# A recurrence beside attention: state rows scanned in pairs, some input products made earlier, and fewer ballast matmuls between the products of a step

## The chip, the cores and the metric

One Trainium2 chip, one core. The metric is the device time of the whole kernel in microseconds. Inputs are 8 sequences of 512 tokens.

## The reference, cut to what matters

```python
h = tok(x)                                  # four attentions of 8 wide heads, (8, 512, 128)
h = h + attn_block(layernorm(h))
h = h + ffn(layernorm(h))
...
x_norm = _ln(x, norm_g, norm_b)             # in attn_block, H = 256, D = 128
xin = jnp.einsum('bsd,hd->sbh', x_norm, W_in)
def res_step(prev, xt):
    new = jnp.tanh(xt + prev @ W_res.T)
    new = LEAK * new + (1.0 - LEAK) * prev  # LEAK = 0.95
    return (new, new)
_, res_states = jax.lax.scan(res_step, h0, xin)
Bm = jnp.einsum('bsd,hd->bsh', x_norm, W_B)
A_bar = jnp.exp(A * delta[..., None])
B_bar = Bm * (1.0 - A_bar) / (A + 1e-08)
def ssm_step(prev, ab_bb): ...              # h = ab * prev + bb, over 512 positions
return readout(res_states) * gate + readout(ssm_states) * (1.0 - gate)
```

`readout` is a layer norm over H, a product with W_ro (128 x 256), and a Gelu.

## The kernel before, in words

The work is cut into 32 tiles of 128 positions of one sequence; tile j is sequence j % 8 of quarter j // 8. Everything is written out in Python, so each engine's order is the order of the calls in its block. The recurrence has 512 steps, which can't be shortened or run side by side. They are grouped into 32 bodies of 16 steps, (t, i) being step t of body i (STEPS, BODIES).

- **Before the steps**: loads, projections and attention of the first eight tiles.
- **Bodies 0 to 23**: 16 steps each, with one tile of attention, its norm and its gate per body beside them. AHEAD = 9 tiles lead.
- **Body 24** (FIRST_DECAY): beside the steps, PE spreads delta over partitions (`spread_delta`, L1680), ACT makes the decays (`decay`, L702), and the scans of the SSM begin.
- **Bodies 25 to 31** (FIRST_READ on): four readout tiles per body, one per four steps, and the rest of the SSM.
- **Tail**: the last eight tiles' readouts at their several stages (`rest_of_readouts`, with `alone=True`).

**A step** (`scan` on each engine). PE adds to a slot of PRE, which already holds the input's part (`fill`): eight products with y16 (four with res_hi, four with res_lo), one with kp's upper half, then 112 columns of zeros (L1490, bodies 0 to 23 only; ballast that adds nothing), four with y_lo, one with kp_lo (L1494). ACT then makes y16 (L637), the f32 state (L638) and kp (L640) from PRE; DVE makes y_lo (L1041) and kp_lo (L1045 or L1048); and the next step begins. PE's other ballast (`pads`, L1529) stands behind the step at hand-set sizes.

**States and their sums.** The leak makes the read state a sum over all earlier ones with factor KEEP = 0.05. ACT writes raw tanh values to `ys`, 16 rows (two halves of H by 8 sequences) of 513 columns, 2052 bytes, each. DVE makes sums in place with one scan per row and quarter (`sigma_row`, L1114): quarters 0 and 1 in bodies 8 to 23, quarter 2 in bodies 24 to 29. The last quarter is done in parts by `half` (64 columns, bodies 28 to 31), `third` (32, body 31) and 32 more a row in the tail, all at L1152, into the places of h_all and gate_all that SP has moved away to `h_last` and `gate_last` (L385 to L396).

**The SSM.** For each of 64 rows, PE makes the input product into PSUM (`feed` on PE, L1669, 128 x 128 f32), DVE multiplies it (`feed_scaled`, L1273) and scans (`recur`, L1289; L1283 and L1286 in the last quarter). Twelve rows are fed in body 24, the others two steps apart from body 25 on. c is the group of eight rows; quarter 0 is c = 0 and 1, 16 rows.

**A readout tile** goes through five stages, `u` being the step within it: PE turns and multiplies the sums (L1691 to L1694), ACT squares (L728), POOL makes the deviation (L513, L516, `r_dev`), DVE scales (L1251), ACT applies Gelu (L717), POOL blends (L539, L540, L502, L506), DVE takes moments (L1320, L1323), POOL their root (L524 to L530), ACT writes (L710), SP stores. On DVE, in a step: `scan`, then `sigma`, then L1251, `recur` or `feed_scaled`, then L1320 at u = 1, which waits for POOL's L506.

```python
                zeros = 112 if i < FIRST_DECAY else 0
                if zeros:
                    t_.matmul(PS[:, t % 2, 0:zeros], ident16[:, :], ballast[:, 0:zeros], start=False, stop=False, skip_group_check=True)
```

## Time and profile before

| | us |
|---|---|
| Three runs | 614.6 (median), 613.83, 616.22 |
| The profiled execution's own time | 613.99 |
| Its span, first to last instruction | 612.10 |
| Until the first tanh of the steps | 113.03 |
| Bodies 0 to 23, 384 steps | 337.96 |
| Body 24 | 18.38 |
| Bodies 25 to 31, to the last tanh | 120.33 |
| Tail | 22.40 |
| Busy over the span: PE, DVE, ACT, POOL | 571.5, 524.4, 430.7, 202.6 |

A row of a timeline is one instruction, or several alike merged (x4): start, length, engine, line, what it writes and reads; in brackets the idle time of the engine just before and who ended it. PE is a matmul, PEld a weight load; ends of matmuls are modelled, so distances are taken from start to start. PEclk is the granted TensorE clock as a share of 2.4 GHz. Matmuls of f32 appear as two instructions each.

### The profile page before, as it was taken

How to read it: one execution, taken by the hardware profiler on the slowest of the kernel's cores; microseconds unless marked ns; L12 is line 12 of the kernel's file. 1: busy time of each engine (PE TensorE's matmuls, PEld its weight loads, DVE VectorE, ACT ScalarE, POOL GpSimd, SP SyncE). 2: the span in 40 equal slices, each digit the busy share in tenths (PEclk: the TensorE clock that was granted, in tenths of full speed). 3: DMA queues.
4: the chain of work that ended last, by engine and by line, in shares of the span. 5: the costliest groups of instructions: out<-in, count | busy, mean ns of one | idle time of the engine just before them, and what ended most of it. 6: DMA issues, size and time to landing. Idle time of an engine off the chain costs nothing.

```text
span 612.1 us, 29176 instructions
## 1 busy us (share of the span) xinstructions
PE 571.5 (93%) x11514; PEld 469.6 (77%) x11514; DVE 524.4 (86%) x2325; ACT 430.7 (70%) x2258; POOL 202.6 (33%) x426
## 2 busy tenths in 40 slices
PE   6888787999999999999999999999999999999972
PEld 2555454788888888888888888888889988998862
DVE  6789886799888889899989999999767788899985
ACT  5587775477777777777777777777758677777764
POOL 1556464011000001110111111011100599898886
PEclk9999999899999999999999999999999999999997
DMA  6000000000000000000000000000020000000001
GB/s 219 2 2 1 2 2 1 3 4 4 4 3 4 3 4 3 4 4 4 4 4 4 4 3 3 4 3 4 3 73 2 3 20 17 20 16 20 16 19 31
DMA packets 8632, 8.35 MB, mean 14 GB/s; under 512 B 944, under 2 KB 7088, under 8 KB 8496
## 3 DMA queue, kind: packets, MB, share of 16 engines
q1 hardware_dynamic: 8208, 5.51, 3.0%
q8 instruction: 90, 1.47, 1.0%
q10 hardware_dynamic: 288, 0.99, 0.5%
q14 instruction: 46, 0.38, 0.2%
HBM read 3.35 MB, written 2.10 MB: 9 GB/s over the span
## 4 chain that ended last, share of the span: by engine, by line
PE 63%; POOL 23%; issue 9%; DVE 2%; DMA 1%; ACT 1%; POOLq 0%; SPq 0%; DVEq 0%
PE PS L1479 20%; PE PS L1529 15%; POOL prob_lo L448 4%; PE PS L1490 4%; POOL r_dev L516 4%; PE PS L1500 4%; POOL ln_small L526 3%; PE PS L1431 2%; PE PS L1438 2%; PE PS L1432 2%; PE PS L1494 2%; PE PS L1486 2%; POOL k L539 2%; POOL k L502 2%; POOL ln_small L530 2%
## 5 line engine op out<-in xcount | busy, mean ns | idle before, releaser
L637 ACT ACTIVATE y<-PS 128x16 f16<-128x16 f32 x512 | 94.3, 184 | 132.3 <-PE PS L1494 121.4
L1529 PE MATMUL PS<-ballast,ident 128*128 128x245 f16 (+7 forms) x648 | 142.7, 296 | 0.0
L1041 DVE TENSOR_TENSOR y_lo<-ys,y 128x16 f16<-128x16 f32 x512 | 96.5, 188 | 49.1 <-ACT ys L638 38.8
L1479 PE MATMUL PS<-y_lo,res_hi 128*128 128x8 f16 x2048 | 128.0, 168 | 2.3 <-DVE y_lo L1041 1.1
L1479 PE MATMUL PS<-y,res_hi 128*128 128x8 f16 x2048 | 127.4, 168 | 0.2
L1479 PEld LDWEIGHTS PS<-y,res_hi 128*128 128x128 f16 x2048 | 96.8, 96 | 38.8 <-ACT y L637 19.0
L1479 PE MATMUL PS<-y,res_lo 128*128 128x8 f16 x2048 | 123.4, 166 | 0.0
L453 POOL TENSOR_TENSOR small<-small,minus_half 128x2 f32<-128x2 f32 x32 | 25.6, 799 | 295.2 <-DVE y_lo L1041 260.3
L638 ACT ACTIVATE ys<-PS 128x16 f32<-128x16 f32 x512 | 99.1, 194 | 0.0
L640 ACT ACTIVATE kp<-PS 128x16 f32<-128x16 f32 x512 | 97.5, 190 | 0.0
L1479 PEld LDWEIGHTS PS<-y_lo,res_hi 128*128 128x128 f16 x2048 | 87.9, 96 | 5.5 <-DVE y_lo L1041 3.2
L923 DVE TENSOR_REDUCE top<-PS 128x1 f32<-128x512 f32 x128 | 87.0, 684 | 4.7 <-PE PS L1406 4.5
L1494 PE MATMUL PS<-kp_lo,carry_id 128*128 128x16 f16 x512 | 87.6, 171 | 0.0
L1479 PEld LDWEIGHTS PS<-y,res_lo 128*128 128x128 f16 x2048 | 87.4, 96 | 0.0
L1486 PE MATMUL PS<-kp,carry_id_top 128*128 128x16 bf16 x512 | 86.5, 169 | 0.0
L1490 PE MATMUL PS<-ballast,ident 128*128 128x112 f16 x384 | 80.3, 209 | 0.0
L590 ACT ACTIVATE prob<-PS 128x512 f32<-128x512 f32 x128 | 77.9, 615 | 1.5 <-PE PS L1418 1.3
L595 ACT ACTIVATE prob_hi<-PS 128x512 f16<-128x512 f32 x128 | 77.8, 615 | 0.0
L955 DVE TENSOR_TENSOR prob_lo<-prob,prob_hi 128x512 f16<-128x512 f32 x96 | 65.4, 683 | 0.0
L1045 DVE TENSOR_TENSOR kp_lo<-kp 128x16 f16<-128x16 f32 x384 | 63.4, 165 | 0.0
L1529 PEld LDWEIGHTS PS<-ballast,ident 128*128 128x128 f16 x648 | 50.1, 98 | 1.0
L1494 PEld LDWEIGHTS PS<-kp_lo,carry_id 128*128 128x128 f16 x512 | 48.9, 96 | 0.0
(240 smaller groups left out, 1483.8 us busy)
## 6 DMA issues: line engine op xcount, KB each, us to landing
ys<-in_x SPq DMA_DIRECT2D x8, 256.0 KB, 7.6
out<-gate_all SPq DMA_DIRECT2D x24, 64.0 KB, 1.5
mats<-in_mats ACTq DMA_DIRECT2D x1, 709.0 KB, 5.0
h_last<-h_all SPq DMA_DIRECT2D x4, 128.0 KB, 2.7
gate_last<-gate_all SPq DMA_DIRECT2D x4, 128.0 KB, 2.9
out<-gate_last SPq DMA_DIRECT2D x16, 32.0 KB, 1.9
rows<-in_rows ACTq DMA_DIRECT2D x1, 257.5 KB, 7.5
wall<-in_wall SPq DMA_DIRECT2D x1, 256.0 KB, 4.8
```

Of the source, the lines that this page charges most:

```text
L590: a_.activation(prob[:, a, :], X[a], ACT.Exp, scale=e_of[j % B])
L595: a_.activation(prob_hi[:, a, :], X[a], ACT.Exp, scale=e_of[j % B]).then_inc(prob_ready, 1)
L637: a_.activation(y16[:, :].rearrange("p (m b) -> p m b", m=NH), pre, ACT.Tanh, scale=back).then_inc(y16_ready, 1)
L638: a_.activation(ys[:, :, bass.ds(i * STEPS + (1 + t), 1)].rearrange("p (m b) o -> p m (b o)", m=NH), pre, ACT.Tanh, scale=back).then_inc(a ...
L640: a_.activation(kp[:, :].rearrange("p (m b) -> p m b", m=NH), pre, ACT.Copy, scale=keep_scale).then_inc(kp_ready, 1)
L923: v.reduce_max(top[:, a:a + 1], X[a], AX_X).then_inc(top_ready, 1)
L1041: v.tensor_tensor(y_lo[:, :], ys[:, :, bass.ds(i * STEPS + (1 + t), 1)].rearrange("p n o -> p (n o)"), y16[:, :], ALU.subtract).then_inc(l ...
L1479: t_.matmul(dst[:, m, :], wts[:, k, m * P:m * P + P], st[:, k * B:k * B + B], start=False, stop=False, skip_group_check=True)
L1486: t_.matmul(dst, carry_id_top[:, :], kp_hi, start=False, stop=False, skip_group_check=True)
L1490: t_.matmul(PS[:, t % 2, 0:zeros], ident16[:, :], ballast[:, 0:zeros], start=False, stop=False, skip_group_check=True)
L1494: t_.matmul(dst, carry_id[:, :], kp_lo[:, :].rearrange("p (m b) -> p m b", m=NH), start=False, stop=True, skip_group_check=True).then_inc( ...
L1529: t_.matmul(at[:, 0:size], ident16[:, :], ballast[:, 0:size], start=False, stop=True, skip_group_check=True)
```

## The change

1. **Fewer zeros.** `chain_zeros(t, i)` leaves out the 112 columns in 108 of the 384 steps of bodies 0 to 23: t = 2 and 8 in all, 1 unless i % 4 is 0, 5, 9 and 10 when i % 4 is 0 or 1, and 6 when it is 1. Ballast at t = 1 goes from 180 to 60 columns, at t = 8 and 9 with i % 4 = 1 from 245 to 180.
2. **The input products of quarter 0** are made in bodies 4 to 11, two per body (t = 10 and 11), in place of ballast, into 256 columns of the bank MISC. ACT copies them in step (2, i + 1) to `last`, the storage of `h_last` and `gate_last`. In body 24 and the first half of 25 PE has no `feed`; `feed_scaled` and `recur` read `last` instead of PSUM. SP moves h_last only when these rows are through.
3. **Two rows per scan.** `ys` is now kept by quarter (the last one in two halves): 16 rows of 128 (or 64) columns, so a step's 16 states are 512 (256) bytes apart. Quarter 2 is summed by `two_rows`, eight scans of 256 columns with a row of factors that is 0 where a row begins; what the quarter before brings in is added to the first states beforehand by `carry_in`, one operation on 16 columns. The last quarter is summed by `two_halves`, eight scans of 128 for its first half (bodies 28 to 30) and eight for its second (tail). `third` is gone.
4. POOL sets the rows of factors at the start.

```diff
-        ys = sb("ys", [P, NH * B, 1 + L])
+        ys = sb("ys", [P, NH * B * L])
...
-        h_last = sb("h_last", [P, B, P])
-        gate_last = sb("gate_last", [P, B, P])
+        last = sb("last", [P, NH, B, P])
+        h_last, gate_last = last[:, 0, :, :], last[:, 1, :, :]
...
+        DRIVE = MISC[:, 512 - NH * P:512]
...
+        def chain_zeros(t, i):
+            if i >= FIRST_DECAY:
+                return 0
+            behind = [2, 8]
+            if i % REGIONS == 0:
+                behind += [5, 9, 10]
+            else:
+                behind += [1]
+            if i % REGIONS == 1:
+                behind += [5, 6, 9, 10]
+            return 0 if t in behind else 112
...
+        FIRST_DRIVE = 4
+
+        def drive_of(i):
+            return i - FIRST_DRIVE if 0 <= i - FIRST_DRIVE < B else None
...
             sp.wait_ge(h_ready, NT)
+            sp.wait_ge(ssm_done, B * NH + EIGHT_FREE)
...
+            g.memset(keep_rows[:, :], KEEP)
+            g.memset(keep_halves[:, :], KEEP).then_inc(keeps_set, 1)
+            pool.wait_ge(keeps_set, 1)
+            for one, size in ((keep_rows, P), (keep_halves, P // 2)):
+                last = g.memset(one[:, :].rearrange("p (n k) -> p n k", k=size)[:, :, 0:1], 0.0)
+            last.then_inc(keeps_set, 1)
...
+            def take_drive(b):
+                act.wait_ge(drive_made, b + 1)
+                a_.activation(last[:, :, b, :], DRIVE.rearrange("p (m n) -> p m n", m=NH), ACT.Copy).then_inc(drive_taken, 1)
+
             for i in range(FIRST_DECAY):
                 for t in range(STEPS):
                     scan(t, i, i % REGIONS)
...
+                    if t == 2 and drive_of(i - 1) is not None:
+                        take_drive(drive_of(i - 1))
...
-                if i == FIRST_DECAY and t == 1:
-                    rows_of(STEPS, 0)
-                if FIRST_READ <= i < FIRST_READ + 5 and t in late:
-                    n = 1 + 3 * (i - FIRST_READ) + late.index(t)
-                    rows_of(STEPS + n // NH, n % NH)
-                if i == BODIES - 4 and t == 7:
-                    dve.wait_ge(halves_moved, 16 * 8)
+                if FIRST_READ <= i and t in late and 3 * (i - FIRST_READ) + late.index(t) < B:
+                    two_rows(NQ - 2, 3 * (i - FIRST_READ) + late.index(t))
+                if (t, i) == (3, BODIES - 4):
+                    carry_in(L - P)
                 if i in (BODIES - 4, BODIES - 3) and t in (7, 14):
-                    half(2 * (i - BODIES + 4) + (t - 7) // 7)
-                if i == BODIES - 2 and t % 4 > 1:
-                    half(4 + t // 4 * 2 + t % 4 - 2)
-                if i == BODIES - 1 and t in (2, 3, 6, 7):
-                    half(12 + (2, 3, 6, 7).index(t))
-                if i == BODIES - 1 and t in (0, 1, 4, 5):
-                    third((0, 1, 4, 5).index(t))
-                if i == BODIES - 1 and t >= 8:
-                    third(4 + t - 8)
-                    if t >= 12:
-                        third(t)
+                    two_halves(0, 2 * (i - BODIES + 4) + (t - 7) // 7)
+                if i == BODIES - 2 and t % 4 == 2:
+                    two_halves(0, 4 + t // 4)
+                if (t, i) == (2, BODIES - 1):
+                    carry_in(L - HALF)
...
+            def carry_in(n):
...
+                v.scalar_tensor_tensor(state(n), state(n - 1), KEEP, state(n), ALU.mult, ALU.add).then_inc(carried, 1)
...
+            def two_rows(q, k):
+                dve.wait_ge(carried, 1)
+                row = k % NH * B + k // NH * 2
+                both = states(q * P)[:, row:row + 2, :].rearrange("p r t -> p (r t)")
+                v.tensor_tensor_scan(both, keep_rows[:, :], both, 0.0, ALU.mult, ALU.add).then_inc(sigma_ready, 2)
...
+            def drive_row(s, c):
+                return last[:, s // 4, c * 4 + s % 4, :] if half_q(c) == 0 else PS[:, 6 + s % 2, 0:P]
...
             def readout(u, n, e, active, alone=False):
-                if 0 in active and alone and u < 2:
-                    for row in range(2):
-                        n_row = (n - SPLIT) * 4 + u * 2 + row
-                        dve.wait_ge(sigma_third, n_row + 1)
-                        last_sums(n_row, HALF + THIRD, THIRD, sigma_last)
+                if 0 in active and alone and u < NH:
+                    two_halves(1, NH * (n - SPLIT) + u)
...
-                zeros = 112 if i < FIRST_DECAY else 0
+                zeros = chain_zeros(t, i)
...
+                if t == 10 and drive_of(i) is not None:
+                    pe.wait_ge(gate_raw, j - 1)
+                    drive(drive_of(i), 0)
+                    pad(MISC, 245)
+                    return
+                if t == 11 and drive_of(i) is not None:
+                    drive(drive_of(i), 1)
+                    return
...
-                if t >= 4:
-                    feed((t - 4) % 8, (t - 4) // 8)
...
-                    if t % 2 == 0 and f < 8 * 2 * NQ:
+                    if t % 2 == 0 and B * NH <= f < 8 * 2 * NQ:
                         feed(f % 8, f // 8)
```

How instructions stand on PE in body 5, from the ballast of step 9 to that of step 10. y, res_hi and res_lo are the recurrence's products, kp and y_lo its small parts, ballast columns that add nothing, xd the fill of PRE, xn with b_t an input product of the SSM. Before:

```order
L1529 MATMUL PS<-ballast,ident 128x245 x2
L1479 MATMUL PS<-y,res_hi 128x8 x4
L1479 MATMUL PS<-y,res_lo 128x8 x4
L1486 MATMUL PS<-kp,carry_id_top 128x2x8
L1490 MATMUL PS<-ballast,ident 128x112
L1479 MATMUL PS<-y_lo,res_hi 128x8 x4
L1494 MATMUL PS<-kp_lo,carry_id 128x2x8
L1529 MATMUL PS<-ballast,ident 128x245 x4
```

And now:

```order
L1583 MATMUL PS<-ballast,ident 128x180 x2
L1533 MATMUL PS<-y,res_hi 128x8 x4
L1533 MATMUL PS<-y,res_lo 128x8 x4
L1540 MATMUL PS<-kp,carry_id_top 128x2x8
L1533 MATMUL PS<-y_lo,res_hi 128x8 x4
L1548 MATMUL PS<-kp_lo,carry_id 128x2x8
L1590 MATMUL PS<-xn,b_t 128x128
L1583 MATMUL PS<-ballast,ident 128x245
```

The zeros before y_lo's products are gone, and one input product has taken the place of three ballasts.

PE in body 24, step 4 and the ballast-free work behind it (delta is spread over the partitions). Before:

```order
L1479 MATMUL PS<-y_lo,res_hi 128x8 x4
L1494 MATMUL PS<-kp_lo,carry_id 128x2x8
L1500 MATMUL PS<-xd,in_t 128x64
L1680 MATMUL PS<-ident,delta 128x128 x2
L1669 MATMUL PS<-xn,b_t 128x128
```

And now:

```order
L1533 MATMUL PS<-y_lo,res_hi 128x8 x4
L1548 MATMUL PS<-kp_lo,carry_id 128x2x8
L1554 MATMUL PS<-xd,in_t 128x64
L1752 MATMUL PS<-ident,delta 128x128 x2
```

The input product at the end of the step has moved to bodies 4 to 11.

DVE in body 31, three steps of a readout tile (keep is the SSM, L1152 the sums, L1251 the scaling). Before:

```order
L1048 SCALAR_TENSOR_TENSOR kp_lo<-PS,setup,kp 128x16
L1152 SCALAR_TENSOR_TENSOR gate_all<-keep_row,ys 128x64
L1273 SCALAR_TENSOR_TENSOR PS<-keep,PS 128x128
L1251 SCALAR_TENSOR_TENSOR k<-PS,r_dev,ro_row 128x128
L1041 TENSOR_TENSOR y_lo<-ys,y 128x16
L1048 SCALAR_TENSOR_TENSOR kp_lo<-PS,setup,kp 128x16
L1152 SCALAR_TENSOR_TENSOR h_all<-keep_row,h_all,ys 128x32
L1251 SCALAR_TENSOR_TENSOR k<-PS,r_dev,ro_row 128x128
L1283 SCALAR_TENSOR_TENSOR keep<-keep,PS 128x64
L1286 SCALAR_TENSOR_TENSOR keep<-keep,PS 128x64
```

And now:

```order
L1103 SCALAR_TENSOR_TENSOR kp_lo<-PS,setup,kp 128x16
L1329 SCALAR_TENSOR_TENSOR PS<-keep,PS 128x128
L1301 SCALAR_TENSOR_TENSOR k<-PS,r_dev,ro_row 128x128
L1096 TENSOR_TENSOR y_lo<-ys,y 128x16
L1103 SCALAR_TENSOR_TENSOR kp_lo<-PS,setup,kp 128x16
L1301 SCALAR_TENSOR_TENSOR k<-PS,r_dev,ro_row 128x128
L1340 SCALAR_TENSOR_TENSOR keep<-keep,PS 128x64
L1343 SCALAR_TENSOR_TENSOR keep<-keep,PS 128x64
```

The scans of sums have left these steps.

## Rows read from the trace of the kernel before

**Rows 1.** Windows by stage: length, busy PE, PEld, DVE, ACT, POOL, PEclk, DMA, GB/s.

```profile
113.03:450.99 337.96, 337.63 (x8237) 286.46 (x8236) 298.66 (x1419) 244.75 (x1443) 36.60 (x48) 1.00 0.02 5
450.99:469.37 18.38, 18.29 (x325) 17.94 (x324) 13.82 (x69) 13.42 (x62) 0.00 (x0) 1.00 0.13 32
469.37:589.70 120.33, 113.83 (x2038) 105.18 (x2039) 106.09 (x491) 86.87 (x547) 97.77 (x252) 1.00 0.06 16
589.70:612.10 22.40, 8.61 (x63) 6.74 (x61) 15.72 (x71) 12.31 (x48) 16.40 (x45) 0.85 0.11 27
```

**Rows 2.** Timeline of ACT, first tanh of steps, bodies 17 to 21: start, length.

```profile
352.31 0.18 ACT L637 ACTIVATE y<-PS 128x16 f16<-128x16 f32 x1
...
359.40 0.18 ACT L637 ACTIVATE y<-PS 128x16 f16<-128x16 f32 x1 [0.46 <-PE PS L1494]
...
360.32 0.18 ACT L637 ACTIVATE y<-PS 128x16 f16<-128x16 f32 x1
...
361.24 0.18 ACT L637 ACTIVATE y<-PS 128x16 f16<-128x16 f32 x1
...
362.10 0.18 ACT L637 ACTIVATE y<-PS 128x16 f16<-128x16 f32 x1
...
366.44 0.18 ACT L637 ACTIVATE y<-PS 128x16 f16<-128x16 f32 x1
...
380.39 0.18 ACT L637 ACTIVATE y<-PS 128x16 f16<-128x16 f32 x1
...
408.48 0.18 ACT L637 ACTIVATE y<-PS 128x16 f16<-128x16 f32 x1
```

**Rows 3.** Timeline of PE in body 17, a late step and one on time.

```profile
359.73 0.24 PE L1479 MATMUL PS<-y,res_hi 128*128 128x8 f16 x4
...
359.96 0.21 PE L1490 MATMUL PS<-ballast,ident 128*128 128x112 f16 x1
360.01 0.24 PE L1479 MATMUL PS<-y_lo,res_hi 128*128 128x8 f16 x4
...
361.48 0.26 PE L1479 MATMUL PS<-y,res_hi 128*128 128x8 f16 x4
```

**Rows 4.** Timeline of body 24, steps without and with an input product on PE.

```profile
454.24 0.18 ACT L637 ACTIVATE y<-PS 128x16 f16<-128x16 f32 x1 [0.17 <-PE PS L1494]
...
455.14 0.18 ACT L637 ACTIVATE y<-PS 128x16 f16<-128x16 f32 x1
...
458.90 0.18 ACT L637 ACTIVATE y<-PS 128x16 f16<-128x16 f32 x1 [0.19 <-PE PS L1494]
...
459.21 0.18 DVE L1041 TENSOR_TENSOR y_lo<-ys,y 128x16 f16<-128x16 f32 x1 [0.20 <-ACT ys L638]
...
459.84 0.27 DVE L1273 SCALAR_TENSOR_TENSOR PS<-keep,PS 128x128 f32<-128x128 f32 x1
460.01 0.18 ACT L637 ACTIVATE y<-PS 128x16 f16<-128x16 f32 x1 [0.20 <-PE PS L1494]
```

**Rows 5.** POOL L516 of eight tiles by line, and waits of DVE in timelines.

```profile
L516 POOL TENSOR_TENSOR r_dev<-r_var,minus_half x8: 705/720/742, 489.1 to 518.9; 128x2 f32<-128x2 f32 x8
...
505.89 0.29 DVE L1320 BATCH_NORM_STATS2 ln_st<-h_all 128x6 f32<-128x128 f32 x1 [0.56 <-POOL h_all L506]
...
521.04 0.45 DVE L1041 TENSOR_TENSOR y_lo<-ys,y 128x16 f16<-128x16 f32 x1 [0.40 <-ACT ys L638]
```

**Rows 6.** The page, costliest groups: the tanh that writes the states.

```profile
L638 ACT ACTIVATE ys<-PS 128x16 f32<-128x16 f32 x512 | 99.1, 194 | 0.0
```

**Rows 7.** Groups of instructions by line and shape, scans of sums on DVE.

```profile
L1114 DVE TENSOR_TENSOR_SCAN ys<-keep_row,ys 128x128 f32<-128x128 f32 x48 | 22.9, 476 | 0.0
...
L1152 DVE TENSOR_TENSOR_SCAN gate_all<-keep_row,ys 128x64 f32<-128x64 f32 x8 | 2.7, 343 | 0.0
```

**Rows 8.** POOL L516 in body 31, by line.

```profile
L516 POOL TENSOR_TENSOR r_dev<-r_var,minus_half x5: 706/707/708, 570.4 to 588.3; 128x2 f32<-128x2 f32 x5
```

**Rows 9.** Timeline of PE in the tail.

```profile
592.49 0.39 PE L1390 MATMUL PS<-ballast,ident 128*128 128x512 f16 x1 [1.93 <-DVE gate_all L1152]
```

118 lines of the change are left out of this document (75 added, 43 removed).

## The prediction

> **What bounds the kernel now.** I read the busy times by stage first [rows 1]. In steps 0 to 383, the 24 bodies beside attention, PE is busy 337.63 of 337.96 us, but much of that is ballast, so busy time doesn't say whether PE or the recurrence is the bound. What says it is the distance between the first tanh (L637) of two steps [rows 2]: 361.24 to 362.10 is 0.865 us, 359.40 to 360.32 is 0.92. A whole body comes close to the first figure: 366.44 to 380.39 is 16 x 0.872. So 0.865 is the latency of one turn of the recurrence (tanh, y_lo, PE, tanh), and I take it as the floor. 384 x 0.865 = 332.2; the stage takes 337.96, so 5.8 us are lost to late steps. In a late one [rows 3] PE starts y's first product at 359.73, 0.33 after the tanh of 359.40; in an on-time one at 361.48, 0.24 after 361.24. y_lo is ready about 0.49 after a tanh (459.21 + 0.18 - 458.90 in [rows 4], the same operations), yet the late step's y_lo products start at 360.01, right behind the 112 zeros of L1490 (359.96): there the zeros are not cover, they are 0.05 us of the path.
>
> In body 24 [rows 4] a step has two spreads of delta and one input product behind the recurrence. With the input product it takes 460.01 - 458.90 = 1.11, without it 455.14 - 454.24 = 0.90. PE is the bound there.
>
> In bodies 25 to 31 the distance of POOL's r_dev [rows 5] is (518.9 - 489.1) / 7 = 4.26 us per tile of readout, four steps. POOL is busy 97.77 of the stage's 120.33 us [rows 1], and its operations on one tile depend on each other. DVE waits for POOL's h_all in about every second tile, 0.56 us in the row shown. So POOL and the steps pace each other, and DVE work counts only where it lies between the release of L1320 and the next square that POOL waits for.
>
> **The change, term by term.** The sum is made against the profiled execution: 613.99 us, its span 612.10.
>
> 1. *Zeros left out in 108 steps of bodies 0 to 23.* A site gives back min(lateness, 0.05). By [rows 2] body 17 (i%4 = 1) takes 352.31 to 366.44, 14.13, which is 0.29 over 16 x 0.865; body 18 (i%4 = 2) 13.95, 0.11 over; bodies 19 and 20 together 380.39 to 408.48, 0.41 over. From the tanh starts within them the named sites hold 0.27 (seven sites), 0.11 (three), and 0.21 (three and five); the rest is at t = 0, 3 and 15, where zeros stay or PE is more than 0.05 late. Times six: 1.6 + 0.7 + 1.3 = 3.6. At one site of the i%4 = 3 bodies DVE's y_lo is late too, so I take 3.4. The shorter ballasts (180 to 60 at t = 1, 245 to 180 at t = 8 and 9) take off the few ns that 0.05 doesn't cover. Ends: 2.8 and 3.6. **-3.4**.
>
> 2. *Eight pairs of input products in bodies 4 to 11.* At t = 10 one replaces three of four 245-column ballasts, 735 columns. 112 columns take 0.05 [rows 3], so these take 0.33, and a product costs the 0.21 by which steps with and without it differ [rows 4]: shorter. At t = 11 one replaces 440 columns, 0.20. That is 0.01 to 0.03 later in a step whose zeros stay: about 0.01 of the path, eight times. ACT's copy of 256 columns stands at t = 2, where ACT has only the three operations of the step; they take at most 3 x 0.19 = 0.57 [rows 6] of 0.865, and while they overlap there is more. Without this cover the copy would cost its own length, some 0.4. Ends 0 and +0.4. **+0.1**.
>
> 3. *Body 24 without the 12 products on PE* [rows 4]. Four steps have a fill of PRE as well, stay bound by PE and lose the product's 0.21: 0.9. Eight others fall from 1.11 towards 0.90, as the step at 454.24: 1.7. What is late next is DVE: y_lo at 459.21 to the end of L1273 at 460.11 is 0.90, nothing to spare, so I take off 0.2 to 0.3. The scan of a row of sums at t = 1 goes and a carry-in of 16 columns comes at t = 2: -0.15. Ends -1.8 and -2.8. **-2.5**.
>
> 4. *Body 25.* The step t = 4 loses a product, -0.22. The scans of sums now cover two rows of 128. From 0.343 us for 64 columns and 0.476 for 128 [rows 7], 2.1 ns a column, a scan of 256 is 0.74, 0.27 more. In the steps t = 6 and 10 DVE's work is 0.63 from y_lo to the end of the SSM scan (459.21 to 459.84 in [rows 4]) and 0.39 for the sums, 1.02 in all, and becomes 1.29: +0.27 each. At t = 2 the load of the Gelu table covers it. **+0.3**.
>
> 5. *Bodies 26 and 27, five more of the long scans*, all behind the bn_stats that waits for POOL. In a tile that waits, the 0.27 lengthens the loop POOL, DVE, steps, ACT, POOL; in its neighbour there are 0.4 us of slack. Ends 0 and 1.35, I take three of five. **+0.8**.
>
> 6. *Bodies 27 (end) to 30.* Seven scans of 0.48 are gone; four of 64 become four of 128, and body 30's eight of 64 become four of 128. A scan is 0.4 of DVE's time net of overlap, and only every second tile waits, so seven can't give more than 7 x 0.4 / 2 = 1.4; the changed sizes about cancel. Part of it lies beside steps that PE bounds. **-0.6**, ends 0 and -1.4.
>
> 7. *Body 31.* Tiles are (588.3 - 570.4) / 4 = 4.48 apart [rows 8], because DVE has four scans of 64 and sixteen of 32 there. All go; POOL's pace of 4.26 is next. Four tiles by 0.22, and the double scans of the last four steps: **-1.0**, ends -0.3 and -1.5.
>
> 8. *Tail.* PE waits 1.93 us for the last sums of the first tile [rows 9]. Two scans of 128 replace four of 32 a tile, about 0.8 us of DVE either way, but the scans of step 15 no longer stand before them. POOL was waiting here too. **-0.6**, ends 0 and -0.9.
>
> At nothing: the four new POOL memsets, which stand before POOL's wait for DVE's first scale (without that wait they would cost what they take, well under 1 us); the memset of ys that goes, on DVE before a wait for PE; and the DMAs of h_last and gate_last, which SP now holds back until the 16 moved rows are through, half a body into body 25. Their data is wanted in body 31, and what is queued behind them on SP are outputs, none before body 26. Were the data late, every engine would stop at tile 24.
>
> Sum: -3.4 + 0.1 - 2.5 + 0.3 + 0.8 - 0.6 - 1.0 - 0.6 = **-6.9**. 613.99 - 6.9 = 607.1; the median of the three runs, 614.6, stands 0.6 above the profiled execution, so I forecast **607.5**.
>
> **A rule against the row.** Row first: y_lo, 0.18 us elsewhere, took 0.45 at 521.04 [rows 5], while POOL's subtraction ran. The Trainium skill ("SBUF — State Buffer", Who interferes with whom) states that a DVE instruction with two SBUF inputs and a GpSimd instruction that reads SBUF shut each other out for their whole length. By that rule, the trace agrees for y_lo. The rule speaks against the long scans, whose inputs both lie in SBUF: each could hold POOL 0.27 longer wherever it falls, up to eight times, 2.2 us instead of the 1.1 of terms 4 and 5. The moved input products gain a second SBUF input as well, but POOL is busy 0.00 in body 24 [rows 1].
>
> **Rivals.**
> *R1, the long scans tax the paced stage.* Terms 4 and 5 reach 1.9, terms 6 and 8 give nothing, term 7 gives 0.6 because POOL's pace is already its bound. For it: POOL is busy 97.77 of 120.33 us even with its idle time in body 25 counted, and its operations wait for one another. Against it: body 31 does follow DVE [rows 8]. 613.99 - 3.3 - 2.5 + 1.3 = 609.5, as a median 610.
>
> *R2, the zeros are not what late steps wait for.* Then PE's next operand would be late as well and term 1 is 0: 611. Against it: no gap between zeros and y_lo in [rows 3]. This is the case in which the change does not do what it says.
>
> *R3, slower: the new layout of the states.* A step's 16 states now go to addresses 512 bytes apart (256 in the last quarter), not 2052. ACT's write and DVE's read of them lie on the path of all 512 steps. Now they cost 0.194 [rows 6] and 0.18 [rows 4], no more than the others, but no row has this distance. It decides from 6.9 / 512 = 13 ns a step; at 25 ns it is 12.8, so 607.5 + 12.8 = 620.3. Against it: neither writes in a pattern that any present row shows to be slow.
>
> *R4, the clock.* It stands at 1.00, 2.4 GHz, in all bodies and at 0.85 in the tail, where PE is busy 8.61 of 22.40 us [rows 1]. With ballast gone PE idles a little more. At 1.2 GHz PE's part of a step, about 0.5 of its 0.865 us [rows 2, 3], doubles: twelve such steps are 6 us, 613.5. The Trainium skill ("TensorE: Matmul & The Clock Gate") states that an idle PE is put back to half rate. Against it: the steps freed were the fullest.
>
> *R5, more than forecast:* terms 6 to 8 near their good ends and 5 near nothing: 604.5.
>
> **From cases to numbers.** Forecast 0.62, R1 0.15, R2 0.07, R3 0.05, R4 0.03, R5 0.08. 0.5% of 614.6 is 3.1 us, about what a measurement of this kernel can tell from no change. Below 611.5 lie the forecast, R1, R5 and most of R2: faster 0.87; the same 0.08; slower 0.05. The range takes R5 and R1 with their spread: 604.5 to 611.0, which leaves out R3, R4 and part of R2.
>
> **What would show it.** Steps 1 to 383 shorter by 3.3 in all, and y_lo's products 0.23 behind y's in the named steps; body 24 at 15.9 instead of 18.38 with steps of 0.90 to 0.93; r_dev 4.3 to 4.4 apart in bodies 26 and 27, at most 4.3 in 31. Wrong would be: a step of 0.88 or more everywhere (R3); 1.00 no longer the clock of a stage (R4); body 24's steps at 1.0 or more, so DVE or the copy is the bound; or the last tanh at 583 but the end not before 607, a tail that POOL sets alone.

## The result, and the profile after

The changed kernel takes 608.78 us (median of 6 runs, 608.09 to 610.26), the one before 614.89 (6 runs). The ratio is 0.990, 95% interval 0.987 to 0.993. Forecast were 607.5, with a range of 604.5 to 611.0. The profiled execution takes 608.47 us, its span is 606.7; before, 613.99 and 612.10. Medians, ranges and ratios below leave out the executions that were over 1.5% slower than their kernel's fastest at a lower granted clock: four of feed_late (627 to 629 us), one each of zeros_alone (619.87) and layout_alone (624.85).

Windows by stage of the changed kernel, cut at the first tanh of bodies 0, 24 and 25 and at the last tanh (columns as in [rows 1]):

```profile
112.50:447.19 334.69, 334.28 (x8127) 284.88 (x8126) 297.12 (x1419) 246.83 (x1451) 36.01 (x48) 1.00 0.01 4
447.19:462.90 15.71, 15.61 (x300) 15.33 (x299) 13.03 (x68) 13.34 (x63) 0.00 (x0) 1.00 0.01 4
462.90:582.80 119.90, 113.34 (x2030) 104.56 (x2031) 103.25 (x465) 86.64 (x547) 97.00 (x251) 1.00 0.10 24
582.80:606.68 23.88, 10.10 (x63) 8.07 (x61) 14.60 (x60) 12.41 (x48) 17.35 (x46) 0.79 0.10 25
```

Against [rows 1], bodies 0 to 23 are 3.27 shorter, body 24 is 2.67 shorter, bodies 25 to 31 are 0.43 shorter (0.17 and 0.68 longer in 25 and in 26 to 27, 0.03 longer in 28 to 30, 1.32 shorter in 31), and the tail is 1.48 longer. The time before the first tanh is 0.53 shorter. That is no work of the change: over all traces of this study it is 112.0 to 113.7 us, and two traces of the changed kernel itself have 112.50 and 112.91. In bodies 0 to 23 two traces of the same program agree within 0.3 us (tail_drive, slow_last and all_three share that stage and take 334.30, 334.02 and 334.03), so a smaller difference there is not read.

Timeline of ACT and PE in the changed kernel's body 17, the step that was late in [rows 3]:

```profile
356.55 0.18 ACT L687 ACTIVATE y<-PS 128x16 f16<-128x16 f32 x1 [0.42 <-PE PS L1548]
...
356.83 0.24 PE L1533 MATMUL PS<-y,res_hi 128*128 128x8 f16 x4
...
357.04 0.17 PE L1540 MATMUL PS<-kp,carry_id_top 128*128 128x16 bf16 x1
357.10 0.26 PE L1533 MATMUL PS<-y_lo,res_hi 128*128 128x8 f16 x4
...
357.42 0.18 ACT L687 ACTIVATE y<-PS 128x16 f16<-128x16 f32 x1
```

The step takes 0.87 instead of 0.92. Nothing stands between kp's product and y_lo's, and y_lo's products start 0.55 after the tanh, no longer behind the zeros: DVE's y_lo is what ends the wait now. Over all 384 steps the tanh starts show step 1 shorter by 0.043 to 0.053 in 22 of the 24 bodies, step 7 by about 0.043 in 18, steps 8 and 9 by 0.055 with i % 4 = 1.

Timeline around the second moved input product (step 11 of body 5): ACT, PE and PE's weight loads.

```profile
205.69 0.30 PEld L1590 LDWEIGHTS PS<-xn,b_t 128*128 128x128 f32 x2
205.72 0.47 PE L1590 MATMUL PS<-xn,b_t 128*128 128x128 f32 x2
205.90 0.18 ACT L687 ACTIVATE y<-PS 128x16 f16<-128x16 f32 x1
205.91 0.10 PEld L1485 LDWEIGHTS PS<-keep,prob_hi 128*128 128x128 f16 x1
...
206.02 0.19 PE L1485 MATMUL PS<-keep,prob_hi 128*128 128x66 f16 x1
...
206.26 0.24 PE L1533 MATMUL PS<-y,res_hi 128*128 128x8 f16 x4
...
206.85 0.18 ACT L687 ACTIVATE y<-PS 128x16 f16<-128x16 f32 x1
```

This step takes 0.95 instead of 0.865. By the starts, the product keeps PE from 205.72 to 206.02, 0.30 us; the ballast of 440 columns that stood there took 0.19 (207.22 to 207.41 in the trace of before). y's product starts 0.36 after the tanh. Six bodies show it (4, 5, 6, 8, 9, 10), 0.085 each; in 7 and 11 two ballasts stood there, and nothing is late.

Groups of the changed kernel by line and shape: the long scans, the paired scans of halves, ACT's copy.

```profile
L1204 DVE TENSOR_TENSOR_SCAN ys<-keep_rows,ys 128x256 f32<-128x256 f32 x8 | 5.4, 681 | 0.0
...
L1211 DVE TENSOR_TENSOR_SCAN ys<-keep_halves,ys 128x128 f32<-128x128 f32 x16 | 6.7, 416 | 0.0
...
L741 ACT ACTIVATE last<-PS 128x256 f32<-128x256 f32 x8 | 3.2, 405 | 0.0
```

POOL's r_dev by line in the changed kernel, tiles 0 to 10 and tiles 22 to 27:

```profile
L566 POOL TENSOR_TENSOR r_dev<-r_var,minus_half x11: 697/704/742, 469.8 to 513.1; 128x2 f32<-128x2 f32 x11
L566 POOL TENSOR_TENSOR r_dev<-r_var,minus_half x6: 704/705/706, 564.8 to 586.4; 128x2 f32<-128x2 f32 x6
```

The same in the kernel before, of which [rows 5] and [rows 8] show parts:

```profile
L516 POOL TENSOR_TENSOR r_dev<-r_var,minus_half x11: 697/706/742, 476.4 to 518.9; 128x2 f32<-128x2 f32 x11
L516 POOL TENSOR_TENSOR r_dev<-r_var,minus_half x6: 706/707/708, 570.4 to 592.4; 128x2 f32<-128x2 f32 x6
```

By the starts to a hundredth, ten tiles took 42.45 before and take 43.40 now. Tiles 22 to 27, beside body 31, took 22.03 and take 21.66. So body 31's steps gained 1.32 us but the readouts only 0.37: r_dev 27, the first of the tail, comes 3.63 after the last tanh (586.43 - 582.80) and came 2.71 after it.

Tail of the changed kernel, timeline of PE:

```profile
586.31 0.27 PE L1768 MATMUL PS<-ident,keep 128*128 128x128 f32 x1
588.90 0.39 PE L1444 MATMUL PS<-ballast,ident 128*128 128x512 f16 x1 [2.31 <-DVE ys L1211]
...
590.41 1.07 PE L1766 MATMUL PS<-ro_pair,keep 128*128 128x129 f32 x4
```

A window that begins where the slower products do:

```profile
590.10:593.10 3.00, 3.00 (x14) 2.60 (x13) 1.88 (x9) 1.96 (x8) 1.59 (x5) 0.50 0.09 22
```

PE stands idle for 2.3 us until DVE has the sums of tile 29, and 0.9 us after it has started again, at 589.80, its clock is granted at 0.50, 1.2 GHz: four read-out products take 1.07 instead of 0.61. The distances of r_dev are 2.63, 3.80, 2.70, 2.64; before they were 3.20, 2.65, 2.76, 2.56.

### The profile page after: what moved, and what is told of

It is laid out like the page before. It is cut to its first block, busy times and chain, and to the rows that moved or that the text cites. A ratio compares the mean times of both kernels' runs of the same rounds, so it can differ in the third digit from the quotient of the medians.

```text
span 606.7 us, 28900 instructions
## 1 busy us (share of the span) xinstructions
PE 565.8 (93%) x11372; PEld 465.7 (77%) x11372; DVE 518.9 (86%) x2287; ACT 432.4 (71%) x2266; POOL 202.3 (33%) x430
## 4 chain that ended last, share of the span: by engine, by line
PE 62%; POOL 24%; issue 9%; ACT 2%; DVE 1%; DMA 1%; POOLq 0%; SPq 0%; ACTq 0%
PE PS L1533 21%; PE PS L1583 14%; POOL prob_lo L498 4%; POOL r_dev L566 4%; PE PS L1554 4%; PE PS L1544 3%; POOL ln_small L576 3%; PE PS L1485 2%; PE PS L1492 2%; PE PS L1486 2%; PE PS L1548 2%; PE PS L1540 2%; POOL k L589 2%; PE PS L1460 2%; POOL k L552 2%
## 5 line engine op out<-in xcount | busy, mean ns | idle before, releaser
L1583 PE MATMUL PS<-ballast,ident 128*128 128x440 f16 (+7 forms) x614 | 135.8, 295 | 0.0
L1533 PEld LDWEIGHTS PS<-y_lo,res_hi 128*128 128x128 f16 x2048 | 85.8, 96 | 6.8 <-DVE y_lo L1096 5.4
L1544 PE MATMUL PS<-ballast,ident 128*128 128x112 f16 x276 | 57.8, 209 | 0.0
L1540 PEld LDWEIGHTS PS<-kp,carry_id_top 128*128 128x128 bf16 x512 | 49.0, 96 | 0.0
```

Of the source, the lines that this page charges most:

```text
L1533: t_.matmul(dst[:, m, :], wts[:, k, m * P:m * P + P], st[:, k * B:k * B + B], start=False, stop=False, skip_group_check=True)
L1540: t_.matmul(dst, carry_id_top[:, :], kp_hi, start=False, stop=False, skip_group_check=True)
L1583: t_.matmul(at[:, 0:size], ident16[:, :], ballast[:, 0:size], start=False, stop=True, skip_group_check=True)
```

## Experiments: the zeros, the products, the states

The first two kernels ask what the zeros are worth, from both sides.

**zeros_back**: the changed kernel with part 1 undone.

```diff
         def chain_zeros(t, i):
...
-            return 0 if t in behind else 112
+            return 112 if i < FIRST_DECAY else 0
...
-                        pad(X[0], 60 if tile else 360)
+                        pad(X[0], 180 if tile else 360)
...
-                            pad(MISC, 180 if fill_at and not behind else 245)
+                            pad(MISC, 245)
```

> The changed kernel with the 112 columns back in all 384 steps and the old ballast sizes, so that only parts 2 to 4 of the change are left. Theory A (a site gives back min(lateness, 0.05) and nothing downstream absorbs it): steps 1 to 383 are longer by 3.4 us in the trace (the 108 sites, seen as step 1 longer by 0.050 in bodies with i % 4 not 0, step 7 by 0.043, steps 4, 5, 8 and 9 by 0.03 to 0.055 with i % 4 = 1), bodies 24 to 31 and tail as in the changed kernel within 0.4, the whole 608.8 + 3.4 = 612.2. Rival B (zeros are cover, and what late steps wait for is something else): steps alike within 0.5 us, 609. Rival C (the gain in steps is taken up behind them by POOL's readouts or the tail): steps longer by 3.4 but the whole by less than 2, 610.5 or less.

**zeros_alone**: the same lines the other way round, in the kernel before.

> The kernel before with part 1 of the change alone (zeros and ballast sizes). Theory A: steps 1 to 383 take 3.8 us less than before (3.4 by the sites of the change, 0.4 more because the six late steps behind the moved input products, 0.085 each, are not there), body 24 as before within 0.1, the whole 614.9 - 3.8 = 611.1. Rival B: 614.5 or more. If the clock rival of the prediction were true in part, the granted clock would fall below 1.00 somewhere in bodies 0 to 23.

Measured: zeros_back 611.34 us (11 runs, ratio to before 0.9945, 0.992 to 0.997), 2.6 above the changed kernel where 3.4 was expected; zeros_alone 612.34 (11 runs, 0.998, 0.995 to 1.000). Window of bodies 0 to 23 in zeros_back:

```profile
112.09:449.88 337.79, 337.45 (x8234) 287.18 (x8234) 297.39 (x1419) 246.94 (x1450) 36.10 (x48) 1.00 0.02 4
```

The same in zeros_alone:

```profile
113.12:448.00 334.88, 334.49 (x8128) 284.04 (x8128) 298.45 (x1419) 244.86 (x1442) 36.62 (x48) 1.00 0.02 5
```

337.79 - 334.69 = 3.10 and 337.95 - 334.88 = 3.07. The 108 sites alone give 3.33 and 3.26; the rest is a few ns the other way in other steps. Rival B falls, and C too in the stages that follow. The clock is 1.00. zeros_alone's whole time stays 1.2 above the expected 611.1. Its trace has PE at half clock from 585.58 for 6.8 us, over the end of body 31 and the tail, and its tail takes 23.5 instead of 22.4.

The six late steps gave 0.5 us away, but zeros_alone, which has none, was not faster than the changed kernel in bodies 0 to 23. Something else in the changed kernel had to give as much back: in the traces of the changed kernel and of zeros_back the median step was 864 ns, in those of before and of zeros_alone 867.

**layout_alone**: the kernel before, with the states by quarter as in the change, 512 bytes apart, and every scan as it was.

```diff
-        ys = sb("ys", [P, NH * B, 1 + L])
+        ys = sb("ys", [P, NH * B * L])
...
+        def states(n):
+            first = n - n % P
+            return ys[:, first * NH * B:(first + P) * NH * B].rearrange("p (r t) -> p r t", t=P)
```

> The kernel before with only the place of the states changed: ys by quarter, 16 rows of 128 columns, so that a step's 16 states are 512 bytes apart and not 2052; all scans are the old ones. Theory H (the new distance shortens the turn of the recurrence by 2 to 3 ns, which explains that the median step is 864 in the changed kernel and in the one with the zeros back, 867 in the one before and in the one with the zeros alone): median step 864, bodies 0 to 23 0.7 to 1.0 us shorter than 337.95, 337.1, the whole 1 us shorter. The prediction's rival R3 (the distance slows the chain): steps 13 ns longer or more. No effect: median 867 and 337.9.

Measured: the median step is 864 ns; bodies 0 to 23 are 0.62 shorter:

```profile
112.82:450.15 337.33, 336.99 (x8237) 285.90 (x8236) 297.57 (x1419) 244.75 (x1442) 36.00 (x48) 1.00 0.02 5
```

Theory H holds, and the prediction's R3 falls. Over the on-time steps of bodies 4 to 23 (those under 870 ns) the mean is 863.5 ns against 865.4; 0.8 of these 2 ns are the tanh that writes the states (192.7 against 193.5), 0.7 DVE's y_lo that reads them (180.0 against 180.7). The 0.62 us is only twice what two traces of one program differ by, but the step times separate all fourteen traces: the twelve with the new layout have means of 862.7 to 863.9, the two with the old one 865.4 and 865.5. The whole, 614.92 (11 runs, 0.999, 0.996 to 1.001), can't show 0.6.

**feed_late**: the changed kernel without part 2.

```diff
         def drive_of(i):
-            return i - FIRST_DRIVE if 0 <= i - FIRST_DRIVE < B else None
+            return None
...
-            sp.wait_ge(ssm_done, B * NH + EIGHT_FREE)
...
                 spread_delta(2 * t + 1)
+                if t >= 4:
+                    feed((t - 4) % 8, (t - 4) // 8)
...
-                    if t % 2 == 0 and B * NH <= f < 8 * 2 * NQ:
+                    if t % 2 == 0 and f < 8 * 2 * NQ:
```

> The changed kernel without part 2: the input products of quarter 0 are again made in bodies 24 and 25, nothing at t = 10 and 11 replaces ballast, ACT makes no copy. Theory A: steps 1 to 383 shorter by 0.5 (the 0.085 at t = 11 of bodies 4, 5, 6, 8, 9 and 10), body 24 longer by 2.6 (18.3), body 25 by 0.1, the whole 608.8 + 2.2 = 611.0. Rival D (DVE with its scans of SSM rows, not PE, held body 24 and it was the scan of sums that went that helped): body 24 stays at 16.5 or less and the whole at 609 or less.

Window of body 24:

```profile
447.17:465.36 18.19, 18.10 (x325) 17.84 (x324) 13.62 (x68) 13.41 (x62) 0.00 (x0) 1.00 0.16 32
```

18.19 against 15.71: rival D falls. Body 25 is 0.22 longer, bodies 0 to 23 are 0.80 shorter, 0.52 of it the six steps; the other 0.3 is spread over all steps and no more than the difference between two traces of one program. Part 2 is worth 1.9 to 2.2 us by the traces. By the medians it would be 3.9: this kernel takes 612.65 us (8 runs, 609.16 to 615.86, ratio 0.996, 0.993 to 0.999) where 611.0 was expected. The excess goes with the clock, 0.976 to 0.984 in the four executions above 613 and 0.991 to 0.994 in the four below; that this comes of part 2 was not tested, and no trace here shows such an execution.

**no_zeros**: the changed kernel without any zeros.

```diff
         def chain_zeros(t, i):
...
-            return 0 if t in behind else 112
+            return 0
```

> The changed kernel with no zeros in any step: the 276 left are out too. Theory A: where PE is on time (y's first product 0.24 to 0.27 behind the tanh) y_lo's products wait for DVE in any case, so the turn stays at 0.863 to 0.865 there; a few late steps gain up to 0.05: t = 12 of six bodies, t = 15 and 0 with i % 4 = 3 and 0: at most 1.0 us in bodies 0 to 23, 333.8. Theory K (the zeros keep PE's granted clock up: they fill 0.05 of the 0.28 between y's and y_lo's products): stretches at 0.50 appear in bodies 0 to 23, each of them costs about 0.5 us per step that it covers, and the times spread upwards. The runs without the moved products and with fewer zeros, which had 4 of 12 executions at 627 to 629 us, speak for some of that.

Measured: bodies 0 to 23 take 333.62, 1.07 less, with the clock at 1.00. The gain is where A put it: 0.048 at t = 12 in six bodies, 0.046 at t = 15 with i % 4 = 3, about 0.02 at t = 1 and 3 with i % 4 = 0, nothing in steps with PE on time. And yet the time is 611.51 (8 runs, 607.82 to 612.74, 0.994, 0.991 to 0.997), nearly 3 above the changed kernel. Windows of the same trace:

```profile
113.63:447.25 333.62, 333.21 (x7851) 281.05 (x7851) 297.11 (x1419) 247.11 (x1450) 36.00 (x48) 1.00 0.01 4
...
533.81:540.64 6.83, 6.83 (x86) 6.50 (x85) 4.59 (x21) 3.75 (x23) 4.44 (x12) 0.50 0.05 12
```

The second row lies in bodies 28 to 30, where this kernel's program is the changed kernel's; they take 53.91 us there, 51.70 in the changed kernel's first trace. So K falls for bodies 0 to 23. Such stretches are not bound to missing zeros: the changed kernel has them too (after_again, next). But the executions differ as a group. The mean granted clock is 0.974 to 0.986 in seven of the eight of no_zeros, 0.994 or more in five of the six of after_again, and 0.993 or more in all six of tail_drive, taken on the same chip. So leaving all zeros out may well make half clock more frequent behind body 24; how it could act from up to 90 us away, no trace shows.

## Experiments: the long scans, the clock and the tail

**after_again**: the changed kernel itself once more.

> The changed kernel itself, unchanged, once more beside the others on one chip. Theory A: bodies 0 to 23 take 334.7 within 0.2, body 24 15.7, bodies 25 to 31 119.9 within 0.2; the time before the first tanh lies anywhere from 112 to 113.7, as in the six traces so far, and is no work of the change. Theory F (the tail's 23.9 us hold one stretch at half clock, 3.4 us at 0.50, that falls on the readouts in one execution and not in another, and 3.6 us by which POOL lags the last tanh): r_dev 27 comes 3.6 after the last tanh again, and the distances of the last r_devs are 2.6, 3.0, 2.7, 2.6 with one of them up to 1.2 longer if the stretch falls there. Rival G (the tail is longer by the paired scans on DVE, in every execution): all distances the same as in the first trace, 3.8 among them, with the clock at 1.00.

Measured: 608.39 us (6 runs, 606.75 to 609.97, 0.988, 0.985 to 0.990). Bodies 0 to 23 take 334.62 and body 24 15.71. The readouts' stage did not repeat within 0.2: body 25 takes 18.34, bodies 28 to 30 take 52.85. Two windows of that trace:

```profile
464.15:467.56 3.41, 3.41 (x38) 2.64 (x38) 1.92 (x8) 2.65 (x10) 0.00 (x0) 0.50 0.00 0
552.89:556.30 3.41, 3.41 (x43) 3.22 (x41) 2.96 (x14) 2.05 (x14) 3.17 (x9) 0.50 0.07 19
```

The tail holds another (from 587.03), but its distances are now 3.29, 2.70, 2.64, 2.50. Rival G falls: the 3.80 of the first trace did not repeat, so it was the clock and not the scans.

**single_rows**: quarter 2 summed by sixteen scans of 128 again, where they stood before; the last quarter's carry-in is split in two parts of 8 columns so that it needn't wait for all of them.

```diff
-                if (t, i) == (2, FIRST_DECAY):
-                    carry_in((NQ - 2) * P)
...
-                if FIRST_READ <= i and t in late and 3 * (i - FIRST_READ) + late.index(t) < B:
-                    two_rows(NQ - 2, 3 * (i - FIRST_READ) + late.index(t))
+                if i == FIRST_DECAY and t == 1:
+                    one_row(STEPS, 0)
+                if FIRST_READ <= i < FIRST_READ + 5 and t in late:
+                    n = 1 + 3 * (i - FIRST_READ) + late.index(t)
+                    one_row(STEPS + n // NH, n % NH)
```

> The changed kernel with quarter 2 summed as before: sixteen scans of 128 columns, at the old steps of bodies 24 to 29, in place of eight of 256; the new layout, the carry-ins (the last quarter's in two parts of 8 columns) and the paired scans of the last quarter stay. Theory A (POOL's chain of readouts sets the stage, and the long scans lengthened it by 0.9 from its first to its eleventh tile): POOL's r_dev from tile 0 to tile 10 takes 42.5 us instead of 43.4, tiles 10 to 23 as in the changed kernel or up to 0.3 longer, so the end comes 0.6 to 0.9 earlier, 608.0. Body 24 is 0.1 longer for the scan at its step 1. Rival E (the seven scans saved in bodies 27 to 30 are worth as much as the long ones cost, as the prediction had it): tiles 10 to 27 0.6 longer, the end the same within 0.3, 608.8.

Measured: 608.48 us (8 runs, 606.46 to 615.23, three of them above 614 at a clock of 0.969 to 0.980; 0.993, 0.989 to 0.998). r_dev 0 to 10 takes 42.35, 1.05 less than with the long scans; 10 to 22 takes 52.61, 1.0 more. That looked like rival E, but a stretch at half clock lay in it:

```profile
547.87:551.28 3.41, 3.41 (x40) 3.28 (x40) 2.80 (x15) 2.19 (x14) 3.25 (x8) 0.50 0.08 25
```

**tail_drive**: zeros out at t = 12 behind the moved product, and nine ballasts in PE's idle time of the tail.

```diff
+            if t == 12 and i % REGIONS != REGIONS - 1 and drive_of(i) is not None:
+                return 0
             return 0 if t in behind else 112
...
                 if 0 in active and u == 1:
+                    if alone and n == IN_SCAN + 1:
+                        pe.wait_ge(kp_lo_ready, L + 1)
+                        for one in range(9):
+                            keep_clock(PS[:, read_banks(n, e), :])
```

> The changed kernel with two edits at separate places. First, at t = 12 of bodies 4, 5, 6, 8, 9 and 10, the steps that come late behind the second moved input product, the zeros are left out: theory A expects those six steps at 0.90 instead of 0.951, 0.3 us in bodies 0 to 23 (334.4). Second, nine ballasts of 512 columns on PE ahead of its wait for the sums of tile 29, into the bank that is free by then, 1.9 us in the 2.3 us in which PE idles there. Theory F: no stretch at 0.50 before PE's last readout, distances of r_dev 2.6, 3.0 or less, 2.7, 2.6, the tail 23.0 or 22.8 instead of 23.9. If nine ballasts are too many, r_dev 28 to 29 grows instead. The whole: 608.8 - 0.3 - up to 1.0 = 607.5 to 608.5.

Measured: 607.53 us (6 runs, 607.29 to 607.96, 0.987, 0.984 to 0.990). The six steps are shorter by 0.048 to 0.050 each; bodies 0 to 23 take 334.30. Timeline of PE in its tail:

```profile
586.70 2.11 PE L1446 MATMUL PS<-ballast,ident 128*128 128x512 f16 x9
589.19 0.39 PE L1446 MATMUL PS<-ballast,ident 128*128 128x512 f16 x1 [0.38 <-DVE ys L1213]
```

And the window from the last tanh to PE's last read-out:

```profile
583.08:596.50 13.42, 10.56 (x72) 7.61 (x70) 10.87 (x45) 8.97 (x39) 11.91 (x30) 1.00 0.08 20
```

The clock is 1.00 to the last read-out, r_dev's distances are 2.63, 2.96, 2.70, 2.64, the tail takes 23.06. With a free clock the second distance is 2.96 in zeros_back too, so the stretch cost 3.80 - 2.96 = 0.84 in the first trace. That the nine ballasts keep the clock up is likely and not shown by this trace: zeros_back and single_rows have no stretch here either, without them.

**all_three**: tail_drive with single_rows' scans.

> The kernel tail_drive with quarter 2 summed by sixteen scans of 128 columns again, as in single_rows. In single_rows' trace r_dev 0 to 10 took 42.35 instead of 43.40, and 10 to 22 took 52.61 instead of 51.62, but a stretch of 3.41 us at half clock lay there (547.87 to 551.28). Theory A (long scans cost, and it was the clock that took it back): without such a stretch 10 to 22 takes 51.6 to 52.0, the end 0.6 to 1.0 earlier than tail_drive's against the last step of body 23, the whole 606.8. Rival E (the scans saved later are worth what the long ones cost): 10 to 22 takes 52.4 or more with the clock at 1.00, the whole 607.5.

Measured: 608.83 us (6 runs, 606.72 to 612.89, 0.990, 0.985 to 0.995). r_dev by line in all_three, tiles 0 to 10 and 10 to 22:

```profile
L568 POOL TENSOR_TENSOR r_dev<-r_var,minus_half x11: 696/706/737, 469.8 to 512.2; 128x2 f32<-128x2 f32 x11
L568 POOL TENSOR_TENSOR r_dev<-r_var,minus_half x13: 704/705/738, 512.2 to 563.9; 128x2 f32<-128x2 f32 x13
```

The same in tail_drive:

```profile
L568 POOL TENSOR_TENSOR r_dev<-r_var,minus_half x11: 696/705/739, 470.1 to 513.4; 128x2 f32<-128x2 f32 x11
L568 POOL TENSOR_TENSOR r_dev<-r_var,minus_half x13: 704/705/737, 513.4 to 565.0; 128x2 f32<-128x2 f32 x13
```

42.38 against 43.34, then 51.73 against 51.63: theory A. The second pair lies at a clock of 1.00; the stretch at half clock that all_three has in body 25 ends before its tile 0. The long scans cost 1.0 us in POOL's chain. What is saved behind them is 0.1, and body 24 is 0.18 longer with the short ones (15.89 against 15.71). So summing quarter 2 by pairs, the first half of part 3, makes the kernel about 0.7 us slower.

Much of that 1.0 is POOL being held while a long scan runs. DVE's scan and POOL's next instruction, with the long scan (changed kernel):

```profile
483.25 0.68 DVE L1204 TENSOR_TENSOR_SCAN ys<-keep_rows,ys 128x256 f32<-128x256 f32 x1
483.49 0.43 POOL L574 TENSOR_TENSOR ln_small<-ln_mv,eps_col 128x1 f32<-128x1 f32 x1
```

The same place with the short one (all_three):

```profile
482.89 0.48 DVE L1206 TENSOR_TENSOR_SCAN ys<-keep_row,ys 128x128 f32<-128x128 f32 x1
483.13 0.22 POOL L576 TENSOR_TENSOR ln_small<-ln_mv,eps_col 128x1 f32<-128x1 f32 x1
```

POOL's instruction is longer by 0.21, as much as the long scan outlasts the short one. The changed kernel has three such places (also at 474.83, 0.67 instead of 0.47, and at 500.82, 0.42 instead of 0.21), and the three tiles in which they lie are each 0.20 longer. That is 0.6 of the 1.0. The other 0.4 lies in tiles in which no instruction of POOL is longer; how it arises was not followed.

Body 25, though, has a stretch at half clock from 463.01 in this trace, and half of the runs are above 610; the gain is one of the trace, not of the median, which is 2.0 above the expected 606.8.

**slow_last**: tail_drive with 224 columns more in each step of body 31.

```diff
+                if i == BODIES - 1 and t > 0:
+                    t_.matmul(PS[:, t % 2, 0:224], ident16[:, :], ballast[:, 0:224], start=False, stop=False, skip_group_check=True)
                 t_.matmul(dst, carry_id[:, :], kp_lo[:, :].rearrange("p (m b) -> p m b", m=NH), start=False, stop=True,
```

> The kernel tail_drive with 224 columns of zeros added on PE ahead of the last product (kp_lo) of each of 15 steps of body 31, 0.09 us each, so that body 31's steps come some 1.4 us later if nothing hides it. Theory L (from body 27 on POOL's chain sets the end, and what steps gain in body 31 comes back as lag of POOL behind the last tanh): the last tanh comes 1.0 to 1.4 later, r_dev 27 comes 2.3 to 2.6 after it instead of 3.63, and the end moves by less than 0.4; the whole 607.5 to 607.9. Rival M (the steps set the end, POOL's lag is constant): the end moves by 1.0 to 1.4, 608.8.

Measured: 608.80 us (5 runs, 0.989, 0.985 to 0.993). From the first step of body 25 the last tanh comes 0.58 later than in tail_drive, r_dev 27 0.44 later, the end 0.43 later. Steps of 0.90 and 0.99 are longer by 0.09 to 0.10, but those at which PE or DVE waits for the readouts take part of it back (1360 to 1251 ns). Neither theory holds as written: in body 31 POOL does not set the pace alone. Steps and readouts hold each other, and three quarters of what the steps lose reach the end.

**more_sites**: tail_drive, zeros out at the further sites that no_zeros showed.

```diff
+            if (t == 15 and i % REGIONS == REGIONS - 1) or (t in (1, 3) and i % REGIONS == 0) or (t, i) == (14, BODIES - 9):
+                return 0
             return 0 if t in behind else 112
```

> The kernel tail_drive with the zeros left out at the sites where the kernel without any zeros was faster, too: t = 15 with i % 4 = 3, t = 1 and 3 with i % 4 = 0, t = 14 of body 23. Theory A: 6 x 0.046 + 0.05 + about 10 x 0.017 + 0.05, bodies 0 to 23 take 333.8 instead of 334.3, 0.5 us less; the median 607.0, which five rounds can just tell from 607.5 at best. Theory K (each site of zeros left out raises the chance of a stretch at half clock): a wider spread of the times than tail_drive's 607.3 to 608.0.

Measured: 608.11 us (6 runs, 605.80 to 611.90, 0.989, 0.984 to 0.993). Bodies 0 to 23 take 333.65, 0.65 less than tail_drive's, and 0.53 of that stands at the named sites, as theory A has it. Its span, 604.0, is the shortest of all traces, but the median is 1.1 above the expected 607.0 and the spread is wider than tail_drive's. Theory K forecast that, yet all_three, with all of tail_drive's zeros, spreads as widely (606.72 to 612.89), so it is not shown.

**best**: more_sites with single_rows' scans, and ballast where PE idled in body 25.

```diff
                         pe.wait_ge(decayed, 12)
+                        keep_clock(PS[:, 3, :])
+                        keep_clock(PS[:, 3, :], 384)
                     if i == FIRST_READ and t == 2:
-                        for n in range(2):
+                        for n in range(4):
```

> All edits that shortened a stage in a trace, together: more_sites (with the ballasts in the tail and the covered moved products) and all_three's sixteen scans of 128 columns; and ballast in the two places of body 25 where PE stood idle ahead of the stretches at half clock at 464.15 and 463.01 (after_again and all_three): 512 and 384 columns behind the fill of step 0, where PE idled 0.43 us, and four times 512 instead of twice in step 2. Theory A with F: bodies 0 to 23 333.6, body 24 15.9, body 25 17.1, r_dev 0 to 10 42.4, 10 to 22 51.4 to 51.8, the tail 23.0; 0.9 us less than more_sites' trace from the first tanh on, no stretch at 0.50 in body 25, and times of 604.5 to 607 with a median of 606. If the stretches in body 25 don't hang on PE's idle time there, times at 610 to 612 stay, as in all_three (three of six) and more_sites.

Measured: 609.14 us (6 runs, 607.40 to 609.37, 0.990, 0.988 to 0.993). Windows of body 25 and of a stretch in bodies 28 and 29:

```profile
462.75:479.86 17.11, 16.95 (x300) 15.28 (x299) 12.78 (x60) 11.88 (x72) 5.25 (x13) 1.00 0.30 59
...
532.61:539.44 6.83, 6.83 (x91) 6.55 (x89) 4.52 (x22) 3.67 (x22) 4.51 (x13) 0.50 0.05 12
```

Body 25 has no half clock and takes what it took in single_rows (17.12), which had no such ballast; so the 0.41 that it is shorter than in more_sites are the scans', and what the ballast does there is not shown by one trace. The expectation fails 70 us later: 6.8 us at half clock make bodies 28 to 30 take 54.24, where all_three took 51.93. Of all kernels tried, tail_drive has the lowest median and the narrowest spread; against the changed kernel's 12 runs (606.75 to 610.26) it is about 0.9 us better. The intervals of the two ratios overlap (0.984 to 0.990, and 0.985 to 0.990 for after_again), so that is all that can be claimed.

## Why the prediction was right, term by term

The whole was: -6.9 forecast for the profiled execution, -5.5 measured. Of the latter 0.5 comes from the time before the steps and 0.6 from the layout of the states, neither of which the sum had; that part of the agreement is luck. The forecast's own terms gave about 4.3 of their 6.9 us, or 5.1 but for a stretch at half clock in the tail.

1. *Zeros*, -3.4: measured -3.1 (-3.3 at the sites alone). Right, by the mechanism named: min(lateness, 0.05), DVE's y_lo next.
2. *Moved input products*, +0.1, ends 0 and 0.4: measured +0.5, outside its ends. The failing sentence is "a product costs the 0.21 by which steps with and without it differ". In body 24 the product stood behind other f32 products, and its starts are 0.11 us apart, 0.22 in all. Between f16 products it takes 0.30: its second half starts 0.19 after its first, as long as one of its weight loads lasts, with short products of 0.025 before it. That the weight load is the reason is read from these starts, not tested. The Trainium skill ("TensorE: Matmul & The Clock Gate", Weight-path perf modes) says that the fast weight load is off for FP32 weights; by that rule, the trace agrees: 188 and 191 ns against 96 for f16 weights. ACT's copies cost nothing: the steps that hold them are as long as without them, within 0.004.
3. *Body 24*, -2.5: measured -2.67, and -2.48 by feed_late. The forecast of 15.9 came out at 15.71.
4. *Body 25*, +0.3: +0.17.
5. *Bodies 26 and 27*, +0.8: +0.68. The scan of 256, put at 0.74, takes 0.681. By single_rows terms 4 and 5 together are worth 1.05 in POOL's chain, forecast 1.1. The size is right, the way to it only in part: 0.6 of it is POOL held by the scan in three tiles, which the prediction had as its rule against the row, at 0.27 and up to eight times, and had left out of the sum. That the two come to nearly the same figure is in part luck.
6. *Bodies 28 to 30*, -0.6: +0.03, and 0.1 by all_three. The step that failed is that every second scan saved counts: the seven saved ones are worth 0.1 together. Why, no experiment isolates. The lower end, 0, held.
7. *Body 31*, -1.0: the steps gain 1.32, the readouts 0.37. The term was counted in steps where POOL's tiles show what reaches the end; but by slow_last POOL is not the only pace there, since three quarters of a loss in steps came through.
8. *Tail*, -0.6: +1.48. It is 0.92 that body 31's steps had run ahead of the readouts, 0.84 of half clock, and -0.3 of the forecast's own work (r_dev 27 to 29: 5.85 before, 5.59 with the clock free). Terms 7 and 8 together, forecast -1.6, are -0.7 with the clock free.
9. *Not in the sum*: the layout of the states, -0.6 in bodies 0 to 23. R3 had the place but the sign was the other.

R1 was half right: the long scans do tax the paced stage, through POOL in part, term 6 does give nothing and term 7 gives the readouts 0.37; but terms 4 and 5 stayed near the sum's values and below 1.9. The profiled execution, 608.47, lies between the forecast's 607.1 and R1's 609.5, and a little nearer to R1. R4 named the right resource at the wrong place: no stretch at half clock lies in bodies 0 to 23 in any trace, even without zeros, while behind body 24 they fall on different places in different executions. "A tail that POOL sets alone" was the failure that the prediction itself named; the last tanh at 582.8 with the end at 606.7 is nearly that.

## What to carry to other kernels

A filler on the critical path is worth min(how late the engine is, its length), site by site; the starts of one recurring instruction give it to 5%, and it does not matter what the engine's busy share says. A product's price holds only among the neighbours that it was read with: move an f32 product between f16 ones and its weight load comes to light. Where steps and a pipeline of another engine pace each other, count a gain at the pipeline's own mark and not at the step's; else the same microsecond is counted once in the stage and is given back in the tail. Before making a DVE instruction longer, look at what POOL does beside it: the length of POOL's own instructions shows whether it is held.
